# A decoder kernel: grouped attention on four row groups, the next layer's fold inside the experts' routing, mask products not held back

## The chip, the core and the metric

One core of one Trainium2 chip runs the whole program. The metric is the device time of one execution in microseconds; less is better. TensorE does the matrix products, VectorE, ScalarE and GpSimd the rest, SyncE (SP) issues most DMAs.

## What is computed

A decoder of four layers on x of shape (16, 64, 256): in each layer an attention, a second attention against ctx_512 (16, 64, 64) and an expert layer, each added to x after a layer norm. Three of these are touched. The grouped attention, which stands in layer 0 and again in layer 3, has no weights:

```python
def _L3_xattn_ref(q, k, v):            # layer 0 has the same one
    B, S, E, QH, KVH = 2, 256, 256, 32, 8
    D = E // QH                        # 8
    G = QH // KVH                      # 4
    ...
    scores = jnp.einsum('bkgsd,bktd->bkgst', qh, kh) / sqrt(D)
    attn = jax.nn.softmax(scores, axis=-1)
    out = jnp.einsum('bkgst,bktd->bkgsd', attn, vh)
```

Layer 2's expert layer picks one of 32 experts for each token; an expert is a 0/1 mask on one shared ternary weight:

```python
probs = softmax(x @ router_w.T); top1 = argmax(probs)
w_scaled = clip(round(weight / 0.5), -1, 1) * scale
out[token] = probs[top1] * x[token] @ (w_scaled * expert_masks[top1]).T
```

Layer 3's attention needs products of its own weights alone (`Wq_nope` with `Wk`, `Wv` with `Wo`). These are the folds; they depend on no activation.

## The kernel before

The 1024 tokens lie on 128 partitions as NT = 8 tiles of 128 tokens (two sequences of 64 each). The program is a row of eleven stages; a stage is a block in which each engine runs its own instruction list, written out by hand, with semaphores between them. `start_loads(n+1)` puts the loads of the next stage on SP's queue at the start of stage n (L3384), so weights are loaded one stage ahead.

`stage_gqa` (L281) does the grouped attention. For each tile j and TensorE:
- `ask(j)` (L319) transposes the tile's queries into bank 6, as eight products with the identity, 32 columns each on two column groups. ScalarE's `query(j)` copies the bank to `qa`.
- `scores(j, gp)` (L329), twice a tile: scores with the queries as stationary operand, on two row groups of which 32 rows each are used, into banks 0 and 1. They serve only for the row maximum, which VectorE's `top` (L481) takes.
- `tops(j)` (L343) turns the maxima into rows of bank 6; `lift` (L304) copies these rows into `qa` beside the queries, one copy of 8 partitions on ScalarE and one on VectorE.
- `cross(j, b)` (L354), twice a tile: transposed scores with the maximum already subtracted (keys times queries, and a row of -1 times the maximum), four products with 40 rows on two row groups, into banks 2 and 3 for b = 0, banks 4 and 5 for b = 1. ScalarE's `exps` (L444) takes the exponential of two banks.
- `weigh(j, b)` (L367) multiplies with the values on four column groups into bank 7; `pull` copies it out, `bring` (L380) transposes back with four full transposes, VectorE's `finish` (L488) divides and adds to x.

TensorE's order in turn t is `scores(t,0)`, `cross(t-1,0)`, `bring(t-2)`, `scores(t,1)`, `cross(t-1,1)`, `ask(t+1)`, `weigh(t-1,0)`, `tops(t)`, `weigh(t-1,1)` (L388 to L410). GpSimd's `spread` (L416) multiplies the keys with a head mask into `kb`. `hold(k, bank, n)` (L1636) is n filler products whose result nobody reads.

`stage_L2_ffn` (L2078) sorts the tokens by expert: logits (`route_logits`, L1622, the router repeated to 128 columns), softmax and choice on VectorE, ranks as products on TensorE, places on VectorE, then eight indirect DMAs by GpSimd scatter the rows to `sorted_in` (semaphore `sent`). SP waits for `sent` and loads the sorted rows back in groups of two tiles. TensorE then runs `turn(b)` (transposes) and `apply(b)` (two blocks of 64 rows, each with its own masked weight) for 24 tiles. VectorE makes the 48 masked weights (L2295) in a ring of six buffers, and waits for `sent` before the first. Between ranks and `turn(0)` TensorE runs 36 fillers and then the folds `fold_nope(g)` (L2136) and `fold_out(g)` (L2146), g = 0 to 3, behind one wait for all of layer 3's attention loads.

`load_L3_attn` (L1309) issues these loads, `load_gqa` (L261) those of the grouped attention.

## Time and profile before

| | us |
|---|---|
| median of 3 runs | 1398.31 (1396.41 to 1400.75) |
| the profiled execution, its own time | 1398.4 |
| its span, first to last instruction | 1396.7 |
| TensorE busy in the span | 1266.5 (91%) |
| VectorE busy | 778.3 (56%) |
| ScalarE busy | 593.1 (42%) |
| GpSimd busy | 371.0 (27%) |

The span falls into stages that follow one another; the two grouped attentions lie at about 220 to 300 and 1275 to 1353 us, the sorted experts at about 1039 to 1129. A share of busy time over the whole span says nothing of a stage, so the rows further down are taken stage by stage. Rows in order of time merge equal instructions that follow one another; the first column is the start, the second the time from the first start to the last end, and square brackets give the idle time in front and what ended it. A product in fp32 is two records on TensorE. A row of busy time gives the stretch and its length, then busy us (and instructions) of PE, PEld, DVE, ACT and POOL, the granted clock of TensorE as a share of 2.4 GHz, the DMA engines' busy share and GB/s.

### The profile page before, as it was taken

Reading aid. Unit: us, or ns where it says so; the run is one execution under the profiler, and the core shown is the slowest. Engines: PE = TensorE matmul, PEld = TensorE weight load, DVE = VectorE, ACT = ScalarE, POOL = GpSimd, SP = SyncE. Lnnn points to the kernel's source line nnn. Section 1 sums busy time; section 2 is a strip of 40 time slices with the busy share of each in tenths; the row PEclk is TensorE's granted clock in tenths of the full one; section 3 lists DMA queues with packets and bytes.
Section 4 is the critical chain, followed back from the end, with each engine's and each line's share of the span. In section 5 each row is a group of like instructions: output and inputs, shape, how many; then the busy total and the mean of one; then the engine's idle time right before and its main releaser. Section 6 shows DMA issues by size and latency. Waiting matters only on the chain. (4 is left out here: it accounts for less than half of the span.)

```text
span 1396.7 us, 29908 instructions
## 1 busy us (share of the span) xinstructions
PE 1266.5 (91%) x12533; PEld 963.0 (69%) x12533; DVE 778.3 (56%) x1473; ACT 593.1 (42%) x1078; POOL 371.0 (27%) x306
## 2 busy tenths in 40 slices
PE   6989998979989998999988888999988968999988
PEld 3469995558977567788857758788775435676555
DVE  4664565553344572633347655888735675863542
ACT  3632334473555474533332441223433363663451
POOL 0154303015641000555520004444202134523000
PEclk9979999988999999999998988999999999999989
DMA  4000003027006000100056080000016312200000
GB/s 115 1 2 4 4 4 122 1 80 151 1 1 204 1 2 1 35 0 1 1 137 180 1 254 1 2 1 2 2 66 207 124 44 50 55 21 31 2 1 31
DMA packets 78421, 67.81 MB, mean 49 GB/s; under 512 B 22344, under 2 KB 74256, under 8 KB 78160
## 3 DMA queue, kind: packets, MB, share of 16 engines
q1 hardware_dynamic: 75472, 63.10, 15.9%
q8 instruction: 100, 1.64, 0.5%
q0 software_dynamic: 768, 2.10, 0.5%
q10 hardware_dynamic: 2048, 0.70, 0.2%
q14 instruction: 33, 0.27, 0.1%
HBM read 53.30 MB, written 8.39 MB: 44 GB/s over the span
## 5 line engine op out<-in xcount | busy, mean ns | idle before, releaser
L1893 PE MATMUL ps<-rounded 128*128 128x512 f32 x384 | 91.3, 393 | 2.0 <-POOL rounded L1924 1.0
L1296 POOL TENSOR_TENSOR fixed<-fixed,cross 128x768 f32<-128x768 f32 x32 | 58.9, 1841 | 109.5 <-DVE cross L1245 109.5
L1210 PE MATMUL ps<-rounded 128*128 128x256 f32 x576 | 79.8, 294 | 6.8 <-DVE rounded L1264 4.1
L1893 PEld LDWEIGHTS ps<-rounded 128*128 128x128 f32 x384 | 70.9, 188 | 20.4 <-POOL rounded L1924 5.4
L1210 PEld LDWEIGHTS ps<-rounded 128*128 128x128 f32 x576 | 73.5, 197 | 10.9 <-issue 4.7
L1924 POOL TENSOR_TENSOR rounded<-weights,rounded 128x256 fp32r<-128x256 f32 x32 | 23.7, 761 | 185.0 <-ACT rounded L1942 185.0
L211 PE MATMUL ps<-fixed 128*128 128x128 f32 x160 | 35.3, 342 | 39.6 <-ACT fixed L199 30.4
L1275 ACT COPY cross<-ps 128x256 f32<-128x256 f32 x32 | 11.9, 373 | 116.0 <-PE ps L1219 116.0
L211 PEld LDWEIGHTS ps<-fixed 128*128 128x128 f32 x160 | 20.4, 166 | 53.5 <-issue 23.0
L1815 DVE SCALAR_TENSOR_TENSOR fixed<-ps,work,fixed 128x256 f32<-128x256 f32 x64 | 28.0, 479 | 51.5 <-PE ps L1725 51.5
L2031 DVE TENSOR_TENSOR work<-work,ps 128x512 f32<-128x512 f32 x32 | 22.0, 688 | 62.1 <-ACT work L1959 60.0
L1219 PE MATMUL ps<-fixed,work 128*128 128x256 f32 x192 | 50.2, 398 | 6.8 <-POOL fixed L1296 6.4
L1580 POOL TENSOR_TENSOR work<-weights,work 64x512 f32<-64x512 f32 x32 | 41.1, 1286 | 56.9 <-DMA work<-work 32.7
L199 ACT ACTIVATE fixed<-fixed 128x256 f32<-128x256 f32 x96 | 51.9, 592 | 8.1 <-DVE fixed L182 8.0
L485 DVE TENSOR_REDUCE work<-ps 128x16 f32<-128x1024 f32 x32 | 39.1, 1222 | 23.6 <-PE ps L337 23.6
L1745 POOL TENSOR_TENSOR rounded<-work,rounded 128x512 fp32r<-128x512 f32 x32 | 41.1, 1299 | 36.8 <-ACT rounded L1776 36.3
L1725 PEld LDWEIGHTS ps<-rounded 128*128 128x128 f32 x384 | 48.9, 199 | 1.1 <-issue 0.7
L1725 PE MATMUL ps<-rounded 128*128 128x256 f32 x384 | 49.3, 290 | 0.0
L188 ACT ACTIVATE fixed<-fixed 128x2 f32<-128x2 f32 x48 | 13.6, 293 | 80.2 <-DVE fixed L172 77.9
L1912 PEld LDWEIGHTS ps<-rounded 128*128 128x128 f32 x384 | 47.0, 192 | 0.5
L1912 PE MATMUL ps<-rounded 128*128 128x256 f32 x384 | 47.2, 283 | 0.0
L1696 PE MATMUL ps<-rounded 128*128 128x512 f32 x192 | 45.5, 392 | 1.7 <-POOL rounded L1736 1.7
(492 smaller groups left out, 3117.3 us busy)
## 6 DMA issues: line engine op xcount, KB each, us to landing
weights<-in_L_ffn_masksT SPq DMA_DIRECT2D x32, 256.0 KB, 6.5
weights<-in_L_ffn_fc_w SPq DMA_DIRECT2D x16, 256.0 KB
weights<-in_L_xattn_Wq SPq DMA_DIRECT2D x2, 2048.0 KB, 9.8
weights<-in_L_xattn_WoT SPq DMA_DIRECT2D x2, 2048.0 KB, 10.2
work<-work SPq DMA_DIRECT2D x64, 64.0 KB, 2.0
sorted_in<-work SPq DMA_DIRECT2D x1, 3072.0 KB, 14.7
work<-sorted_in SPq DMA_DIRECT2D x12, 256.0 KB, 2.8
sorted_out<-work SPq DMA_DIRECT2D x12, 256.0 KB, 2.2
```

Source lines behind the costliest of these rows:

```text
L199: nc.scalar.activation(to, of, ACT.Identity, bias=k.nshift[:, j:j + 1], scale=k.nrstd[:, j:j + 1]).then_inc(s["n_normed"], 1)
L211: last = nc.tensor.transpose(k.ps[:, banks[i % 2], (2 * c + jj) * P:(2 * c + jj + 1) * P], k.h[:, 2 * i + jj, c * P:(c + 1) * P], k.ident)
L485: nc.vector.tensor_reduce(mx[:, j % 2, gp, :], ps[:, 0:2, :].rearrange("p a (n t) -> p (a n) t", t=SEQ), AX.X, ALU.max).then_inc(s["maxed" ...
L1210: last = nc.tensor.matmul(seen[:, a, :], m[:, u % 2, c, a, :], of[:, c, part * D:(part + 1) * D], start=c == 0 and n == 0, stop=c == KC - ...
L1219: last = nc.tensor.matmul(ps[:, 2, 0:D], c1[:, v // 4, a, :], ro[:, v % 2, a, :], start=a == 0, stop=a == 2)
L1296: nc.gpsimd.tensor_tensor(ro[:, v % 2, :, :], ro[:, v % 2, :, :], sn, ALU.add).then_inc(s["roped"], 1)
L1580: last = nc.gpsimd.tensor_tensor(qb[64:128, 2 * (u % 2) + e, tok], cs[made, v % 2, :], turned_sn[made, v % 2, :], ALU.add)
L1696: last = nc.tensor.matmul(ps[:, 2 * m + half, :], a[:, q % 2, c, :], b[:, c, half * BANK:(half + 1) * BANK], start=c == 0 and part == 0, s ...
L1725: last = nc.tensor.matmul(ps[:, 4 + i, jj * D:(jj + 1) * D], a[:, (e - 1) % 2, c, j * P:(j + 1) * P], b[:, (e - 1) % 2, c, :], start=c == ...
L1745: nc.gpsimd.tensor_tensor(a_rest[:, e % 2, m, tok], act1[:, (4 * e + 2 * m + half) % 3, :], a_top[:, e % 2, m, tok], ALU.subtract).then_in ...
L1893: last = nc.tensor.matmul(ps[:, 2 * (n % 2) + i, :], a[:, q % 2, i, c, :], b[:, c, half * BANK:(half + 1) * BANK], start=c == 0 and part = ...
L1912: last = nc.tensor.matmul(ps[:, 4 + i, jj * D:(jj + 1) * D], a[:, (e - 1) % 2, c, j * P:(j + 1) * P], b[:, (e - 1) % 2, c, :], start=c == ...
```

## The change

In the grouped attention (both uses):
- Keys and queries are laid out in four row groups of 32 partitions in place of two: group r holds in its rows 4 to 19 the 16 numbers of a pair of heads for each of `b`, and in rows 0 to 3 the place for the negated maxima. The rows of ones and the mask now come by DMA: `load_gqa` issues 42 DMAs where it issued 19.
- The normed tile is first copied into a padded buffer `hp` (tile 0 by VectorE, the others by GpSimd); `ask` is then four full transposes, and waits for the padded copy. It moves ahead of `cross(t-1,1)`.
- `scores` uses 64 rows in each of its two row groups; `tops` is eight products on four column groups, with the negated identity `minus`.
- `lift` is four copies of 4 partitions, two on each engine; on VectorE it moves behind `front`, the statistics of the next layer norm.
- `cross` is four products on four row groups into banks 2 to 5, of which b has its half. It waits for the exponentials before it (`2j + b`), where it waited for those before that.
- At the stage's start the fills with -1 and the mask's products go; fills of `hp` with zeros and the first padded copy come.

In the sorted experts: the logits use the 32 router columns once; `fold_nope(0)` moves between logits and ranks, behind a wait for its two loads, which are now the first that `load_L3_attn` issues; the other folds follow the ranks, `fold_out` behind a wait for two further loads; 20 fillers then follow in place of 36 before. VectorE doesn't wait for `sent` any more.

```diff
+    ones, one_hot = d["const_rope64"], d["const_gmask"]
+    for r in range(4):
+        pair, at = r % 2, 32 * r
+        for first, n in ((at, 4), (at + 20, 12)):
+            eng.dma_start(w.keys[first:first + n, :, :, :].rearrange("p b j t -> p (b j) t"),
+                          bass.AP(tensor=ones.tensor, offset=ones.offset, ap=[[0, n], [0, 2 * NT], [1, SEQ]])).then_inc(sem, 16)
+        for first, n, row, col in ((at + 4, 16, 16 * pair, 0), (at + 20, 12, 0, 4)):
+            eng.dma_start(w.gmask[first:first + n, :].rearrange("p (b n) -> p b n", b=2),
+                          bass.AP(tensor=one_hot.tensor, offset=one_hot.offset + 8 * row + col, ap=[[8, n], [0, 2], [1, 4]])).then_inc(sem, 16)
+        for b in range(2):
+            eng.dma_start(w.gmask[at + 2 * b:at + 2 * b + 2, :],
+                          bass.AP(tensor=one_hot.tensor, offset=one_hot.offset + 64 * (4 * b + 2 * pair), ap=[[64, 2], [1, 8]])).then_inc(sem, 16)
+    return 16 * (16 + 2 + 4 * 6)
...
     def lift(eng, copy, s, j, half):
         eng.wait_ge(s["topped"], j + 1)
-        copy(qa[lows[half], j % 3, :, :, :].rearrange("p b g q -> p b (g q)"), bc(ps[lows[half], 6, 0:D], 1, 2)).then_inc(s["lifted"], 1)
+        for low in lows[2 * half:2 * half + 2]:
+            copy(qa[low, j % 3, :, :, :].rearrange("p b g q -> p b (g q)"), bc(ps[low, 6, 0:D], 1, 2)).then_inc(s["lifted"], 1)
+
+    def padded(copy, s, j):
+        copy(hp[:, j % 3, :, :, 4:20], k.h[:, j, :].rearrange("p (g r d) -> p g r d", g=GQA_G, r=4)).then_inc(s["padded"], 1)
...
             def ask(j):
                 if j:
                     pe.wait_ge(s["queried"], j)
+                    pe.wait_ge(s["padded"], j)
+                else:
+                    pe.wait_ge(s["padded0"], 1)
+                if j >= 2:
+                    pe.wait_ge(s["lifted"], 4 * (j - 1))
                 for g in range(GQA_G):
-                    for half in range(2):
-                        at = 64 * g + 32 * half
-                        last = nc.tensor.matmul(ps[64 * half:64 * half + 32, 6, g * P:(g + 1) * P], k.h[:, j, at:at + 32],
-                                                k.ident, start=True, stop=True, tile_position=(0, 64 * half))
+                    last = nc.tensor.transpose(ps[:, 6, g * P:(g + 1) * P], hp[:, j % 3, g, :, :].rearrange("p r d -> p (r d)"), k.ident)
                 last.then_inc(s["asked"], 1)
...
+                pe.wait_ge(s["minus"], 1)
                 for gp in range(2):
-                    for half in range(2):
-                        last = nc.tensor.matmul(ps[lows[half], 6, gp * P:(gp + 1) * P], mx[:, j % 2, gp, 8 * half:8 * half + 8],
-                                                k.ident, start=True, stop=True, tile_position=(0, 64 * half + 32))
+                    for r in range(4):
+                        last = nc.tensor.matmul(ps[lows[r], 6, gp * P:(gp + 1) * P], mx[:, j % 2, gp, 4 * r:4 * r + 4],
+                                                minus, start=True, stop=True, tile_position=(0, 32 * r))
                 last.then_inc(s["topped"], 1)
 
             def cross(j, b):
-                pe.wait_ge(s["lifted"], 2 * j + 2)
-                if j:
-                    pe.wait_ge(s["expd"], 2 * j - 1 + b)
-                for pair in range(2):
-                    for half in range(2):
-                        rows = slice(64 * half, 64 * half + 40)
-                        last = nc.tensor.matmul(ps[:, 2 + 2 * b + half, pair * D:(pair + 1) * D],
-                                                kb[rows, 2 * j + b, 2 * pair:2 * pair + 2, :].rearrange("p n t -> p (n t)"),
-                                                qa[rows, j % 3, b, :, :].rearrange("p g q -> p (g q)"),
-                                                start=True, stop=True, tile_position=(64 * half, 0))
+                pe.wait_ge(s["lifted"], 4 * j + 4)
+                if 2 * j + b:
+                    pe.wait_ge(s["expd"], 2 * j + b)
+                for r, rows in enumerate(groups):
+                    pair = r % 2
+                    last = nc.tensor.matmul(ps[:, 2 + r, b * D:(b + 1) * D],
+                                            kb[rows, 2 * j + b, 2 * pair:2 * pair + 2, :].rearrange("p n t -> p (n t)"),
+                                            qa[rows, j % 3, b, :, :].rearrange("p g q -> p (g q)"),
+                                            start=True, stop=True, tile_position=(32 * r, 0))
                 last.then_inc(s["crossed"], 1)
...
+                if t + 1 < NT:
+                    ask(t + 1)
                 if 1 <= t <= NT:
                     cross(t - 1, 1)
-                if t + 1 < NT:
-                    ask(t + 1)
...
+            nc.gpsimd.memset(hp[:, 1:3, :, :, :], 0.0).then_inc(s["hzero"], 1)
             pool.wait_ge(w.sem, w.loaded)
-            pool.wait_ge(s["minus"], 2)
-            pool.wait_ge(s["masked"], 3)
             spread(0)
+            pool.wait_ge(s["hzero"], 1)
+            for j in range(1, 3):
+                padded(nc.gpsimd.tensor_copy, s, j)
...
                 spread(j)
+                if j + 1 < NT:
+                    pool.wait_ge(s["asked"], j - 1)
+                    if j == 2:
+                        pool.wait_ge(s["padded0"], 1)
+                    padded(nc.gpsimd.tensor_copy, s, j + 1)
...
-                nc.scalar.activation(pT[:, b, :, :].rearrange("p m q -> p (m q)"),
-                                     ps[:, 2 + 2 * b:4 + 2 * b, :].rearrange("p a q -> p (a q)"), ACT.Exp,
-                                     scale=scale).then_inc(s["expd"], 1)
+                nc.scalar.activation(pT[:, b, :, :],
+                                     ps[:, 2:6, b * D:(b + 1) * D], ACT.Exp, scale=scale).then_inc(s["expd"], 1)
...
+            nc.vector.memset(hp[:, 0, :, :, :], 0.0).then_inc(s["hzero0"], 1)
+            dve.wait_ge(s["hzero0"], 1)
+            nc.vector.tensor_copy(hp[:, 0, :, :, 4:20], k.h[:, 0, :].rearrange("p (g r d) -> p g r d", g=GQA_G, r=4)).then_inc(s["padded0"], 1)
+            nc.vector.tensor_scalar(minus, k.ident, -1.0, None, ALU.mult).then_inc(s["minus"], 1)
...
                 if t < NT:
                     top(t, 1)
-                    lift(dve, nc.vector.tensor_copy, s, t, 1)
                 if t >= 2 and t % 2:
                     front((t - 3) // 2)
+                if t < NT:
+                    lift(dve, nc.vector.tensor_copy, s, t, 1)
...
+    w.keys_sem, w.values_sem = k.nc.alloc_semaphore("L3_keys_weights"), k.nc.alloc_semaphore("L3_values_weights")
+    eng.dma_start(w.kT, d[p + "WkT"]).then_inc(w.keys_sem, 16)
+    eng.dma_start(w.qnT, d[p + "Wq_nopeT"]).then_inc(w.keys_sem, 16)
+    eng.dma_start(w.vT, d[p + "WvT"]).then_inc(w.values_sem, 16)
+    eng.dma_start(w.wo, d[p + "Wo"].rearrange("(h p) d -> p h d", p=P)).then_inc(w.values_sem, 16)
+    eng.dma_start(w.all, d[p + "Wall"].rearrange("(c p) s -> p c s", p=P)).then_inc(sem, 16)
     eng.dma_start(w.rot, d[p + "Wq_rot"][0:P]).then_inc(sem, 16)
     eng.dma_start(w.rot_low, d[p + "Wq_rot"][P:192]).then_inc(sem, 16)
-    eng.dma_start(w.all, d[p + "Wall"].rearrange("(c p) s -> p c s", p=P)).then_inc(sem, 16)
-    eng.dma_start(w.qnT, d[p + "Wq_nopeT"]).then_inc(sem, 16)
-    eng.dma_start(w.kT, d[p + "WkT"]).then_inc(sem, 16)
-    eng.dma_start(w.vT, d[p + "WvT"]).then_inc(sem, 16)
-    eng.dma_start(w.wo, d[p + "Wo"].rearrange("(h p) d -> p h d", p=P)).then_inc(sem, 16)
...
             pe.wait_ge(w.sem, w.loaded)
-            route_logits(k, pe, w.router, E, s["logits"])
+            for j in range(NT):
+                for c in range(KC):
+                    last = nc.tensor.matmul(ps[:, 6 + j // 4, (j % 4) * P:(j % 4) * P + E], k.hT[:, c, j * P:(j + 1) * P], w.router[:, c, :],
+                                            start=c == 0, stop=c == KC - 1)
+            last.then_inc(s["logits"], 1)
+            pe.wait_ge(k.next.keys_sem, 32)
+            fold_nope(0)
             pe.wait_ge(s["order"], 3)
             pe.wait_ge(s["sel"], 1)
...
             last.then_inc(s["ranks"], 1)
-            hold(k, 4, 36)
-            pe.wait_ge(k.next.sem, k.next.loaded)
+            for g in range(1, 4):
+                fold_nope(g)
+            pe.wait_ge(k.next.values_sem, 32)
             for g in range(4):
-                fold_nope(g)
                 fold_out(g)
+            hold(k, 4, 20)
             pe.wait_ge(s["noped"], 4)
             pe.wait_ge(s["pms"], 4)
             turn(0)
@@ -2198,6 +2229,7 @@
                 for made, rows, half in ((k.next.nope, slice(0, P), 0), (k.next.low, slice(64, P), 1)):
                     ins = nc.scalar.copy(made[rows, 2 * g:2 * g + 2, :].rearrange("p u d -> p (u d)"), ps[rows, 2 + g % 2, half * D:half * D + D])
                 ins.then_inc(s["noped"], 1)
+            for g in range(4):
                 act.wait_ge(s["pm"], g + 1)
                 nc.scalar.copy(k.next.pm[:, 2 * g:2 * g + 2, :].rearrange("p a d -> p (a d)"), ps[:, g % 2, :]).then_inc(s["pms"], 1)
             copy_turned(0)
@@ -2287,7 +2319,6 @@
             chain.step(nc.vector.tensor_reduce(passed[row], past[row], AX.X, ALU.add))
             nc.vector.tensor_scalar(table[row], passed[row], E - 1.0, float(KC * D), ALU.min, ALU.mult).then_inc(s["table"], 1)
             dve.wait_ge(s["table"], 1)
-            dve.wait_ge(s["sent"], 16 * NT)
```

## Rows read from the trace of the kernel before

**Rows 1.** Order of time, turn t=5 of the first attention: start us, us, engine, line.
```profile
263.08 1.13 PE L337 MATMUL ps<-work 32*128 32x256 f32 x8
...
264.26 1.23 DVE L485 TENSOR_REDUCE work<-ps 128x16 f32<-128x1024 f32 x1 [1.28 <-PE ps L337]
...
265.21 0.66 PE L383 MATMUL ps<-fixed,work 128*128 128x128 f32 x4
265.33 1.02 ACT L448 ACTIVATE work<-ps 128x1024 f32<-128x1024 f32 x1 [1.52 <-PE ps L361]
...
265.80 1.13 PE L337 MATMUL ps<-work 32*128 32x256 f32 x8
...
266.76 0.42 DVE L495 TENSOR_TENSOR fixed<-fixed,work 128x256 f32<-128x256 f32 x1
...
266.86 1.14 PE L361 MATMUL ps<-work 40*128 40x256 f32 x8
...
267.92 0.95 PE L325 MATMUL ps<-fixed 128*32 128x128 f32 x13
...
269.04 0.58 ACT L441 COPY work<-ps 96x512 f32<-96x512 f32 x1 [2.69 <-PE ps L325]
...
269.72 0.61 PE L350 MATMUL ps<-fixed,work 128*8 128x128 f32 x8 [0.30 <-issue]
270.37 0.70 DVE L306 COPY work<-ps 8x512 f32<-8x512 f32 x1 [2.05 <-PE ps L350]
...
270.59 0.64 PE L375 MATMUL ps<-work 128*32 128x256 f32 x8 [0.27 <-ACT work L448]
...
271.16 1.13 PE L337 MATMUL ps<-work 32*128 32x256 f32 x8
```

**Rows 2.** Busy time per engine, granted clock (PEclk), DMA, over the first attention's loop.
```profile
231.00:291.00 60.00, 55.07 (x548) 33.52 (x548) 33.97 (x56) 31.68 (x41) 2.05 (x3) 1.00 0.11 35
```

**Rows 3.** Order of time, the edges of the first attention stage.
```profile
220.87 0.91 DVE L501 MEMSET weights<- 32x1024 f32 x1 [1.67 <-PEq L78]
...
224.93 1.13 PE L337 MATMUL ps<-work 32*128 32x256 f32 x8
...
238.84 1.13 PE L337 MATMUL ps<-work 32*128 32x256 f32 x8
...
285.95 1.13 PE L361 MATMUL ps<-work 40*128 40x256 f32 x8
```

**Rows 4.** Order of time, the sorted experts up to their first tile.
```profile
1039.75 5.34 PE L1626 MATMUL ps<-fixed 128*128 128x128 f32 x32 [0.93 <-PEq L78]
...
1050.11 0.37 PE L2160 MATMUL ps<-work 128*128 128x256 bf16 x1 [5.02 <-DVE work L1606]
...
1061.23 1.54 PE L2141 MATMUL ps<-weights 128*128 128x64 f32 x13 [1.08 <-DMA fixed<-in_L_attn_kv_norm_w]
...
1068.05 5.14 SPq L2221 DMA_DIRECT2D work<-sorted_in  x5
...
1072.17 0.85 PE L2120 MATMUL ps<-fixed,work 128*128 128x128 f32 x6 [0.72 <-issue]
```

**Rows 5.** One line's operations (mask products): ns min/median/max, first and last start.
```profile
L2295 DVE TENSOR_TENSOR work<-weights,fixed x48: 691/693/695, 1069.1 to 1107.5; 128x512 f32<-128x512 f32 x48
```

**Rows 6.** Busy time, clock, DMA share and GB/s while the next layer's weights load.
```profile
1041.00:1047.00 6.00, 4.09 (x28) 3.90 (x27) 2.60 (x6) 0.42 (x1) 0.34 (x1) 0.84 1.00 337
```

**Rows 7.** The page's DMA issues: count, KB each, median us from issue to landing.
```profile
work<-sorted_in SPq DMA_DIRECT2D x12, 256.0 KB, 2.8
```

**Rows 8.** Order of time, GpSimd's scatter and gather beside VectorE's operations.
```profile
1054.52 1.74 DVE L2286 TENSOR_TENSOR work<-work 1x1536 f32<-1x1536 f32 x1
1054.92 2.43 POOL L2245 DMA_INDIRECT sorted_in<-fixed,work  x1 [13.57 <-DVE work L2283]
...
1115.29 0.95 POOL L2250 DMA_INDIRECT work<-sorted_out,work  x1 [0.30 <-issue]
1115.60 0.48 DVE L2299 SCALAR_TENSOR_TENSOR fixed<-work,fixed 128x256 f32<-128x256 f32 x1 [7.44 <-DMA work<-sorted_out,work]
```

35 lines of the change are left out of this document (14 added, 21 removed).

## The prediction

> **What bounds the kernel now.** I read the order of time in three places: one turn of the grouped attention's loop, that stage's edges, and the start of the sorted experts. The busy time of two stretches, one line's operations and one row of the DMA issues answer what is left.
>
> In the loop [rows 1] one turn lasts 271.16 - 263.08 = 8.08 us, and TensorE starts a new group as soon as the last one lets it: `scores` 1.06 (265.80 to 266.86), `cross` 1.06 (266.86 to 267.92), `bring` with four full transposes 0.59 (265.21 to 265.80), `weigh` 0.57 (270.59 to 271.16). Two `scores`, two `cross`, one `bring` fill 4.83. `ask` from 267.92 is in VectorE's and ScalarE's chain: its end lets ScalarE copy the queries (269.04 to 269.62), that lets `tops` start (269.72), that the lift (270.37). VectorE's `top` takes 1.23, the exponentials 1.02. So TensorE bounds the loop, with about half a us of waiting in front of `tops`. The granted clock is full there (1.00, the 2.4 GHz level) [rows 2].
>
> The edges: the loop begins at 224.93, its third turn at 238.84 (13.9 us for two turns, the first behind fillers, the second behind the load of the exponential's table), and the last tile's `cross` is at 285.95 [rows 3]. In between there are five full turns (t = 2 to 7): 238.84 + 5 x 8.08 = 279.24.
>
> In the sorted experts [rows 4] the chain is: logits to 1045.1, VectorE's routing, ranks on TensorE at 1050.11, places, the scatter, its landing, `turn(0)`. The folds for the next layer begin at 1061.23, when the last of that layer's loads lands, and run on one after another until `turn(0)` at 1072.17. After it the 48 mask products (0.693 each, 1069.1 to 1107.5 [rows 5]) set the pace: 38.4 us over 47 steps, 0.817 a product, 1.63 for the two of a tile.
>
> **Part 1, the attention, step by step.** Seen from TensorE's turn:
> - `cross`: four products, before on two row groups (two rounds, 1.06), now on four (one round). No row of before has four row groups of 128 columns. From below by the count of rounds: half the streaming goes. `weigh` has the same moving width (256) and one round on four column groups, 0.57 [rows 1], so a round beyond the first costs 1.06 - 0.57 = 0.49 at most. Bounds: 0.57 and 1.06. I take 0.63, near `weigh`, because the pair on two row groups already runs together (the same 1.06 does for four products).
> - By the Trainium skill, TensorE: Matmul & The Clock Gate, Part 3 (Measured speedup vs the span model), four row groups gave 3.07 times, not 4. By it the round would be about 0.1 longer, the turn about 0.25, the sum about 2.5 smaller. No run here shows it yet.
> - `ask`: eight narrow products become four full transposes, as `bring`: 0.59 for 0.68 or so. It moves ahead of `cross(t-1,1)`, which takes ScalarE's copy off the way to `tops`.
> - Lift: two copies become four, two on each engine. A copy of 4 partitions is as long as one of 8, so VectorE's becomes 0.70 x 2 = 1.40 [rows 1].
> - Padded copies on GpSimd: some 256 elements a tile; its eight spreads leave it idle for most of the loop. Nothing, as long as it is a tile ahead; exposed it would be about a us a turn.
> - `cross` now waits for the preceding exponentials, since all four banks are shared. Between two `cross` there are `bring`, `scores`, `ask`, 2.2 us, against 1.02: free in the loop.
>
> The new turn, from `scores(t,0)` = 0: `cross(t-1,0)` 1.06 to 1.69, `bring` to 2.28. `top(t,0)` starts at 1.18 (as 264.26 after 263.08) and ends at 2.41, and only then may `scores(t,1)` start: 2.52, a wait that is new, to 3.58. `ask` to 4.17, query copy to 4.87. `cross(t-1,1)` to 4.80, exponentials 4.92 to 5.94, `weigh` to 5.37. `top(t,1)` ends at 4.99 (VectorE does the finish of an older tile first, from 2.45: it takes 1.31, as from `bring`'s end at 265.87 to 267.18), so `tops` goes at 5.37 to 5.94. `weigh(t-1,1)` 5.98 to 6.55. The turn is **6.55**, 1.53 less. Lifts: 6.05 to 7.45; they release `cross(t,0)` at 7.56, it is due at 6.55 + 1.06 = 7.61. So there is 0.05 of room: VectorE's lift is what comes next.
>
> Five turns give 5 x 1.53 = 7.65. The first two together give 0.5: the lift is exposed there (0.4 to 0.5 lost) and ScalarE's table load goes 0.6 later, while the earlier `ask` and shorter `cross` give 1.4 back. The last turn loses 0.9: it has no `scores` after the lift, and VectorE's norm statistics (1.05) now stand ahead of the lift, so the last tile's `cross` comes 7.6 after the turn's start, not 6.71. The tail behind it, two `cross` and two exponentials in series, is 0.2 shorter. Start: the fills and mask products go (0.91 of VectorE for 1024 columns [rows 3]), but `ask(0)`, which before waited for nothing in the stage, waits for a fill of 512 (half of that, 0.46) and a copy of 256 columns (0.42, as 266.76): 1.0 later with the releases, and with half the matmuls 0.4 to 0.9 shorter: 0.3 lost. One stage: 7.65 + 0.5 - 0.9 + 0.2 - 0.3 = 7.15. **Two stages: 14.3.**
>
> The load of the stage has 23 more DMAs on SP's queue. At some 0.35 to 0.7 us to issue each that is 8 to 16 us; it is issued a whole stage earlier, and nothing in the rest of those stages starts that soon. Nothing; exposed it would be those 8 us once.
>
> **Part 2, the fold and the logits.** Logits with 32 columns in place of 128: the rate there is 5.34/32 = 0.167 a record over both clock levels; the fold's products, with 64 columns, take 1.54/13 = 0.118, tail included [rows 4]. The stretch from 1041 shows 337 GB/s [rows 6]: 2.1/0.337 = 6.2, landed at 1047.3 to 1048. The fold takes 1.9, so it ends at 1049.5 or so, ahead of the ranks at 1050.11. Queued behind it on TensorE are the ranks, and VectorE waits for those. Bounds: 0.4 gained, 1.5 lost; I take 0. The other folds and 20 fillers end by about 1067. Then `turn(0)` no longer waits for folds but for the first sorted rows, issued at 1068.05 [rows 4] and some 3 us to landing (2.8 [rows 7]): 1071.1 for 1072.17, **1.0 gained**. But TensorE now idles for 3 to 4 us before it, where the folds ran right up to it. If the clock falls to its 1.2 GHz level, the first tiles cost up to 1.5 more. I take 1.0 lost.
>
> **Part 3, the mask products ahead.** Six buffers, so six products (4.4 us) can be done early. Before, they were done at 1073.9, and the seventh waits for the first tile's products at 1074.2: the gain is 0.3 unless the first tile comes earlier. The 42 others go at 0.817 from then. What it can cost is the scatter: [rows 8] the first scatter DMA took 2.43 on GpSimd, from 1054.92, beside a VectorE product with two SBUF inputs that ended at 1056.26; but the gather's took 0.95 with such an operation of 0.48 inside it, neither one longer. So an issue that starts within a product may wait for its end (0.3 on average, at most four issues) and one that is under way does not: 0 to 4.2 (all six products), I take 0.8. The Trainium skill, SBUF — State Buffer (SBUF: two separate sides), says that of a VectorE operation with two SBUF inputs and a GpSimd operation that reads SBUF, the one that starts first has the port pair for its whole length; the first row agrees, the gather's do not. By it the scatter would be some 4 us later.
>
> Parts 2 and 3: 1.0 + 0.3 - 1.0 - 0.8 = -0.5.
>
> **Sum.** 14.3 - 0.5 = 13.8. The profiled execution took 1398.4 (span 1396.7 and 1.7 around it), 0.1 above the median of 1398.31. 1398.4 - 13.8 = **1384.6**.
>
> **Rivals.**
> - *Four row groups run as two rounds.* Then `cross` stays at 1.06; the order alone gives a turn of 7.2, 0.88 less, so 5 x 0.88 + 0.5 - 0.9 - 0.1 = 3.9 a stage less 0.3: 7.2 for both. 1391.7. For it: no row shows four. Against: the column groups. 12%.
> - *Scatter and products block each other* (mechanism above, in full). Each issue waits for a product and the clock falls as well: 4 us more than I took: 1388.6. For it the 2.43, against it the gather. 14%.
> - *The lift sets the turn.* If VectorE's two copies or an exponential over four banks are 0.3 longer, `cross` waits 0.3 a turn: 5 x 0.3 x 2 = 3: 1387.6. 10%.
> - *Slower: the clock falls inside the loop.* The shorter groups leave TensorE waiting in front of `scores(t,1)` and `weigh`. At 1.2 GHz each round streams twice as long: 2 x 1.91, 2 x 1.06, five of 1.0: 10.9 a turn. Above a share of (8.08 - 6.55)/(10.9 - 6.55) = 35% of the loop at that level the change loses; with both loops at it throughout, 1384.6 + 10 x 4.35 = 1428. Against: 1.00 now [rows 2], with the half us of waiting per turn there already. 4%.
> - *It doesn't do what it says*: padded copies or added loads bound the stage instead, and the gain is gone: 1398. 4%.
>
> Forecast 56%, between 1381 and 1387.
>
> **Numbers.** The range reaches from 1380.5 (both folds' gains, no cost of parts 2 and 3) to 1391.5 (most of the first three rivals). Within 0.3% (4.2 us, about what can be told from no change): 1394 to 1402.5. Faster 0.87, same 0.08, slower 0.05.
>
> **What would show it.** Right: a turn near 6.5 between two `scores(t,0)`, the `cross` group 0.6 long with its four weight loads together, `scores(t,1)` released by `top`, ranks at 1050, `turn(0)` after its rows' landing. Wrong: `cross` still 1.06, a wait on the lift in front of `cross(t,0)`, scatter issues of over 1 us, or a low granted clock in either loop. What would make the number wrong most easily is the 0.05 us of room at the lift, and the clock at `turn(0)`.

## The result and the profile after

| | before | changed |
|---|---|---|
| median, same chip | 1397.36 us (1392.70 to 1400.75, 4 runs) | 1377.30 us (1375.72 to 1380.95, 4 runs) |
| ratio, 95% interval | 1 | 0.9856 (0.9828 to 0.9884) |

The change is faster by 20 us, with 16 to 24 in the interval. Forecast were 13.8 us less and a range down to 1380.5; the time lies 3.2 us below that range. The profiled execution took 1375.72.

The changed kernel's page: span, busy time, and the granted clock in 40 slices (tenths).

```profile
span 1374.0 us, 29841 instructions
...
PE 1243.2 (90%) x12453; PEld 947.3 (69%) x12453; DVE 790.8 (58%) x1487; ACT 602.8 (44%) x1094; POOL 376.5 (27%) x320
...
PEclk9989999989999999999998989999996999999989
```

The slice of 6 at about 1030 us is the start of the sorted experts, at half clock.

The changed kernel in order of time, one steady turn of the first attention (answers to [rows 1]): `scores` is L358, `cross` L380, `bring` L402, `ask` L346, `weigh` L394, `tops` L370, the lift L321, `top` L509.

```profile
247.68 1.42 DVE L321 COPY work<-ps 4x512 f32<-4x512 f32 x2 [0.17 <-PE ps L370]
...
248.32 1.13 PE L358 MATMUL ps<-work 64*128 64x256 f32 x8
...
249.38 0.31 PEld L380 LDWEIGHTS ps<-work 32*128 32x128 f32 x8 [0.33 <-DVE work L321]
249.38 0.71 PE L380 MATMUL ps<-work 32*128 32x256 f32 x8
249.50 1.22 DVE L509 TENSOR_REDUCE work<-ps 128x16 f32<-128x1024 f32 x1 [0.41 <-PE ps L358]
...
250.03 0.65 PE L402 MATMUL ps<-fixed,work 128*128 128x128 f32 x4
...
250.87 1.14 PE L358 MATMUL ps<-work 64*128 64x256 f32 x8 [0.19 <-DVE work L509]
...
251.94 0.66 PE L346 MATMUL ps<-fixed,work 128*128 128x128 f32 x4
...
252.52 0.71 PE L380 MATMUL ps<-work 32*128 32x256 f32 x8
...
253.17 0.64 PE L394 MATMUL ps<-work 128*32 128x256 f32 x8
253.30 1.02 ACT L473 ACTIVATE work<-ps 128x1024 f32<-128x1024 f32 x1
...
253.62 0.62 PE L370 MATMUL ps<-work 128*4 128x128 f32 x16
...
254.31 1.42 DVE L321 COPY work<-ps 4x512 f32<-4x512 f32 x2 [1.04 <-PE ps L370]
...
254.38 0.64 PE L394 MATMUL ps<-work 128*32 128x256 f32 x8
...
254.95 0.49 PE L358 MATMUL ps<-work 64*128 64x256 f32 x2
```

The turn is 254.95 - 248.32 = 6.63 us. `cross` holds TensorE 0.65 (249.38 to 250.03). The wait forecast as new is there, 0.19 behind `top`. So is the lift's: 247.68 + 1.42 = 249.10, and `cross` starts at 249.38, just as `scores` lets it go. The loop's clock stayed full (answers to [rows 2]):

```profile
230.00:283.00 53.00, 46.15 (x525) 25.93 (x525) 39.64 (x71) 36.90 (x53) 4.20 (x6) 1.00 0.05 17
```

The changed kernel in order of time, the sorted experts up to the first tile (answers to [rows 4] and [rows 8]).

```profile
1024.55 7.01 PE L2183 MATMUL ps<-fixed 128*128 128x32 f32 x32 [0.93 <-PEq L78]
...
1032.00 3.02 PE L2165 MATMUL ps<-weights 128*128 128x64 f32 x16 [0.44 <-DMA weights<-in_L_attn_Wq_nopeT]
...
1036.57 0.37 PE L2190 MATMUL ps<-work 128*128 128x256 bf16 x1 [1.55 <-DVE work L1630]
...
1041.38 2.44 POOL L2277 DMA_INDIRECT sorted_in<-fixed,work  x1 [15.23 <-DVE work L2315]
...
1045.74 0.69 DVE L2326 TENSOR_TENSOR work<-weights,fixed 128x512 f32<-128x512 f32 x1 [1.03 <-issue]
...
1046.88 0.69 DVE L2326 TENSOR_TENSOR work<-weights,fixed 128x512 f32<-128x512 f32 x1 [0.44 <-issue]
1047.72 2.90 DVE L2326 TENSOR_TENSOR work<-weights,fixed 128x512 f32<-128x512 f32 x4
1047.91 1.33 POOL L2277 DMA_INDIRECT sorted_in<-fixed,work  x1 [0.30 <-issue]
...
1049.55 1.17 POOL L2277 DMA_INDIRECT sorted_in<-fixed,work  x1 [0.30 <-issue]
...
1054.71 4.03 SPq L2253 DMA_DIRECT2D work<-sorted_in  x5
...
1057.73 1.20 PE L2144 MATMUL ps<-fixed,work 128*128 128x128 f32 x6 [1.76 <-DMA work<-sorted_in]
...
1060.98 1.45 DVE L2326 TENSOR_TENSOR work<-weights,fixed 128x512 f32<-128x512 f32 x2 [10.36 <-PE ps L2155]
```

Counted from the first logit product, before and after: logits 5.34 and 7.01 us long, ranks at 10.36 and 12.02, first scatter at 15.17 and 16.83, `turn(0)` at 32.42 and 33.18. Between these two executions the stage lost 2.6 us.

**Where the 22.7 us between the two profiled spans lie.** Counted from TensorE's first product of one stage to that of the next, some 9 of them lie in stages whose code is the same in both kernels. The first attention, to the next stage's logits, went from 79.4 to 72.2, near the 7.15 less of the forecast. But the L0 experts behind it took 107.9 for 111.1, the L1 stage 144.7 for 145.6, the last layer's attention 143.4 for 145.3, and the L0 attention ahead of it all 200.8 for 203.9. This count puts the start of each grouped attention, up to its own first product, into the stage ahead of it, and that start is 5.17 us with the new code for 3.69 (first attention; 2.73 for 1.73 at the second). Counted from the last product ahead of the stage, the first attention gave 5.8 us (77.3 for 83.1) and the second 7.7 (72.5 for 80.3), and the unchanged code is nearly 12 us shorter, 4.6 of it in the L0 attention (195.6 for 200.2).

Three theories. A: my sum stands, and what the unchanged stages gave is not the change's. B: a shorter attention moves the low stretches of TensorE's clock in what follows. C: one execution's luck. Every kernel below has a trace, and so one more execution of the unchanged stages.

### The profile page after: what moved, and what is told of

Same layout as the page of the kernel before. It is cut to its first block and busy times, and to the rows that moved or that the text cites. A ratio compares the mean times of both kernels' runs of the same rounds, so it can differ in the third digit from the quotient of the medians.

```text
span 1374.0 us, 29841 instructions
## 1 busy us (share of the span) xinstructions
PE 1243.2 (90%) x12453; PEld 947.3 (69%) x12453; DVE 790.8 (58%) x1487; ACT 602.8 (44%) x1094; POOL 376.5 (27%) x320
## 3 DMA queue, kind: packets, MB, share of 16 engines
q1 hardware_dynamic: 78096, 63.63, 16.3%
## 5 line engine op out<-in xcount | busy, mean ns | idle before, releaser
L1917 PE MATMUL ps<-rounded 128*128 128x512 f32 x384 | 91.1, 393 | 2.0 <-POOL rounded L1948 1.0
L1298 ACT COPY cross<-ps 128x256 f32<-128x256 f32 x32 | 11.9, 372 | 115.3 <-PE ps L1242 115.3
L509 DVE TENSOR_REDUCE work<-ps 128x16 f32<-128x1024 f32 x32 | 39.2, 1224 | 18.2 <-PE ps L358 17.6
```

Of the source, the lines that this page charges most:

```text
L509: nc.vector.tensor_reduce(mx[:, j % 2, gp, :], ps[:, 0:2, :].rearrange("p a (n t) -> p (a n) t", t=SEQ), AX.X, ALU.max).then_inc(s["maxed" ...
L1917: last = nc.tensor.matmul(ps[:, 2 * (n % 2) + i, :], a[:, q % 2, i, c, :], b[:, c, half * BANK:(half + 1) * BANK], start=c == 0 and part = ...
```

## The experiments

**b_attn, b_experts: the halves of the change.** b_attn is the kernel before with the diff's attention part (its functions `load_gqa` and `stage_gqa`); b_experts is the kernel before with the rest.

> The kernel before with the attentions' part of the change alone (four row groups, padded copies, earlier ask, new loads); the sorted experts, their fold and the order of the last layer's loads are as before. Theory A, my forecast's own sum: 14.3 us less than before (about 1383), so the 20 us come mostly from elsewhere. Theory B, the trace of after: the two attention stages give 13.9 to 14 and the stages that were not changed give the rest (L0 attention 4.7, L0 experts 3.8, L3 attention 2 to 3 shorter), because TensorE's low-clock stretches fall elsewhere once the attention is shorter; then this kernel alone is 20 to 23 us faster than before (about 1375 to 1377). Theory C: the shorter unchanged stages are one execution's luck in where the low clock falls; then this kernel's profile has L0 attention and L0 experts nearer to before, and its median gain is 14 to 17.

Measured: 1377.98 against 1395.01, ratio 0.9890 (0.9866 to 0.9915): 15.3 us less, 11.9 to 18.7.

> The kernel before with the rest of the change alone: logits of 32 columns, the first fold ahead of the ranks, loads reordered, mask products not waiting for the scatter. The attentions are as before, so its trace up to 1040 us is a second execution of unchanged code. My forecast: 0.5 us slower. By the trace of after (that stage 92.85 us for 90.2): 2.6 slower. A rival: the reordered loads make the last layer's attention shorter by 2 to 3, so the sum is 0. Theory C (luck of the low clock): its stages ahead of 1040 us differ from before's by some us in places although nothing is changed there; otherwise each agrees within 0.5.

Measured: 1396.58 against 1395.01, ratio 1.0000 (0.9976 to 1.0023).

So the attention is the whole gain, and the other two parts are worth nothing within some 3 us. The interval holds A's 14.3 and C's 14 to 17, and not B's 20. C is right about one stage: the L0 attention took 203.9 in before and 200.2 in b_experts, with the same code. It comes in two courses: with low clock from 60 us after its start for 17 us and also at 16, or only from 56 to 59 on, for 14 or 17 us. Of all 14 profiled executions three took the long one: before, b_dense (204.2, old attention) and a_logits128 (205.2, new). What separates the two courses, 3.7 us between before and b_experts, is the execution's own. The L0 experts' are not, as the table further down shows, and there B holds, with a smaller amount.

**b_order: the loop's order alone.**

```diff
+                if t + 1 < NT:
+                    ask(t + 1)
                 if 1 <= t <= NT:
                     cross(t - 1, 1)
-                if t + 1 < NT:
-                    ask(t + 1)
...
-                    lift(dve, nc.vector.tensor_copy, s, t, 1)
                 if t >= 2 and t % 2:
                     front((t - 3) // 2)
+                if t < NT:
+                    lift(dve, nc.vector.tensor_copy, s, t, 1)
```

> The kernel before with only the order of the attention's loop as changed: ask(t+1) ahead of cross(t-1,1) on TensorE, VectorE's norm statistics ahead of the lift; cross on two row groups, fills, masks and loads as before. By my forecast's working for a second round in cross, the order alone gives a turn of 7.2 for 8.08, so 5 x 0.88 x 2 = 8.8 less the last turn's 0.9 x 2: 7 us faster than before. If instead the turn's gain came from the row groups (two cross of 1.06 become 0.64, 0.84 a turn) and the order gives only what is left of 1.45, the turn is 7.47 and the kernel 4 to 5 us faster. If both are needed together (VectorE's chain sets the turn unless cross is short), the turn stays within 0.2 of 8.08.

Measured: 1386.93 against 1396.30, ratio 0.9931 (0.9905 to 0.9957), 9.6 less (6.0 to 13.3). b_order in order of time, TensorE, one turn:

```profile
241.96 1.13 PE L337 MATMUL ps<-work 32*128 32x256 f32 x8
...
246.73 1.13 PE L361 MATMUL ps<-work 40*128 40x256 f32 x8
247.79 0.64 PE L375 MATMUL ps<-work 128*32 128x256 f32 x8
248.26 0.61 PE L350 MATMUL ps<-fixed,work 128*8 128x128 f32 x8
248.99 0.64 PE L375 MATMUL ps<-work 128*32 128x256 f32 x8
249.56 0.70 PE L337 MATMUL ps<-work 32*128 32x256 f32 x4
```

The turn is 249.56 - 241.96 = 7.60, not 7.2: of the 1.45 that a turn gained, 0.48 is the order and 0.97 the rest of the attention's change: the row groups with their two shorter `cross` (0.82), and what goes with them. From the last product ahead of the stage to the next stage's first logits it takes 81.55 for 84.41, and 77.55 for 80.25 at the second attention (b_fill's, below, whose attentions are as before): 5.6 us for both. That is nearer to the second expectation (a turn of 7.47, 4 to 5 us) than to my 7; the whole came out lower still, with an end of its interval at 6.0.

**a_logits128, a_fold_late, a_fold_late2: what the routing's start costs.** a_logits128 is the changed kernel with the logits on 128 columns:

```diff
-            for j in range(NT):
-                for c in range(KC):
...
-            last.then_inc(s["logits"], 1)
+            route_logits(k, pe, w.router, E, s["logits"])
```

> The changed kernel with the router's logits computed on 128 (repeated) columns again, all else as changed. In the trace of after, the stage's first 24 us ran at the 1.2 GHz level and the logits took 7.0 us for 5.34 before. If the narrow products keep the clock low: the logits take 5.3, the level is back at 1.00 within them, the ranks come 1.7 earlier, the folds run at full clock, and the whole is 1.7 to 3 us faster than the changed kernel (1374 to 1375.6). If the clock is low there for another reason (what ran before the stage), the logits get longer, by up to 0.5 us, and the whole is the same or slower by 0.5.

Measured: 1377.56 against 1395.01, ratio 0.9872 (0.9848 to 0.9897); not told apart from the changed kernel's. a_logits128 in order of time:

```profile
1028.12 5.45 PE L1650 MATMUL ps<-fixed 128*128 128x128 f32 x32 [0.93 <-PEq L78]
...
1036.96 3.01 PE L2165 MATMUL ps<-weights 128*128 128x64 f32 x16 [3.39 <-DMA weights<-in_L_attn_Wq_nopeT]
...
1039.90 0.39 PE L2186 MATMUL ps<-work 128*128 128x256 bf16 x1
```

The logits are back at 5.45. Over all profiled executions they took 5.3 to 5.5 with 128 columns and 6.2 to 7.0 with 32. But the ranks came only 0.24 earlier, at 11.79 after the first logit product, now held by something else: `fold_nope(0)` waited 3.39 for its load, ran 3.0 at half clock, and the ranks stood behind it with no idle time.

a_fold_late moves that fold behind the ranks, to the other three, with 36 fillers for 20 ahead of `turn(0)`; a_fold_late2 is the same with 16.

```diff
-            pe.wait_ge(k.next.keys_sem, 32)
-            fold_nope(0)
             pe.wait_ge(s["order"], 3)
...
-            for g in range(1, 4):
+            pe.wait_ge(k.next.keys_sem, 32)
+            for g in range(4):
                 fold_nope(g)
...
-            hold(k, 4, 20)
+            hold(k, 4, 36)
```

> The changed kernel with logits of 128 columns and fold_nope(0) behind the ranks (with the other folds), 36 fillers for 20 ahead of turn(0). In a_logits128 fold_nope(0) waited 3.4 us for its load at 8.84 after the first logit product, ran at the 0.5 level, and the ranks stood behind it until 11.79, for 10.36 in before. Theory: ranks at 10.4 to 10.5, the scatter's end 1.3 earlier, turn(0) at 31.6 instead of 32.9, the seventh mask product at 33.7 instead of 35.1 (full level at turn(0)), so 1.3 us faster than a_logits128 (about 1376). Rival: the rows' landing or the sorted rows' load sets turn(0) all the same: no change.

Measured: 1380.30 against 1396.30, ratio 0.9896 (0.9869 to 0.9923). a_fold_late in order of time, TensorE:

```profile
1034.04 0.37 PE L2184 MATMUL ps<-work 128*128 128x256 bf16 x1 [5.02 <-DVE work L1630]
...
1035.21 11.52 PE L2165 MATMUL ps<-weights 128*128 128x64 f32 x61
...
1051.35 7.72 PE L1663 MATMUL ps<-fixed 128*128 128x512 bf16 x35 [0.16 <-issue]
1058.90 0.82 PE L2144 MATMUL ps<-fixed,work 128*128 128x128 f32 x6
```

The ranks are at 10.47, 1.3 earlier, as expected; `turn(0)` is at 35.3, not 31.6, because my 36 fillers stood in front of it for 7.7 us.

> a_fold_late with 16 fillers in place of 36 ahead of turn(0). There the ranks came at 10.47 and the last scatter issue ended at 27.14 after the first logit product, as expected, but the fillers ran from 27.8 to 35.3 and turn(0) stood behind them. With 16 they end at 31.2 to 31.4; turn(0) goes with its rows' landing at 31.6 to 31.9, and the seventh mask product at 33.7 to 34.0, for 35.1 in a_logits128 and a_sent: 1.2 us faster than these by the trace in this stage, at most 1376 to 1377 for the whole (less than the timing can tell from the changed kernel). Rival: the load of the first sorted rows lands later than 31.9 whatever the scatter does; then turn(0) stays near 32.9.

Measured: 1376.03 against 1395.88, ratio 0.9856 (0.9826 to 0.9886), again not told apart from the changed kernel. `turn(0)` at 33.24 and the seventh mask product at 35.31: neither is earlier than a_logits128's 32.89 and 35.12. Not the rows' load (the rival) held it: TensorE was never idle there. Four folds behind the ranks ended at 30 us, and the 16 fillers (3.4) behind them set `turn(0)`. The earlier ranks were given back to the folds. So the fold ahead of the ranks takes 1.3 from the routing and gives them back later; between the two places there is nothing to gain as long as folds and fillers fill the time up to `turn(0)`. The kernel with the late fold and no fillers was not run. In a_logits128 `turn(0)` came 4.4 us after the last scatter issue's end (28.49); by that the rows of a_fold_late2 (27.02) were there at an estimated 31.4, nearly 2 us before its `turn(0)`.

**a_sent: the wait for the scatter put back.**

```diff
             dve.wait_ge(s["table"], 1)
+            dve.wait_ge(s["sent"], 16 * NT)
```

> The changed kernel with VectorE's wait for the end of the scatter put back ahead of the mask products. Contention theory at its full price (4 us): 4 us faster than the changed kernel, scatter issues of 0.95. By the trace of after (issues of 0.96 to 1.33, 0.6 over in all): the scatter ends 0.6 earlier, turn(0) 0.6 earlier, but the six products are late and the seventh is where it was: within 0.5 us of the changed kernel. My forecast's numbers: 0.8 back and 0.3 lost, so 0.5 faster.

Measured: 1378.94 against 1395.01, ratio 0.9894 (0.9870 to 0.9917). a_sent in order of time, its sixth and seventh scatter issues and first mask products:

```profile
1047.21 0.96 POOL L2277 DMA_INDIRECT sorted_in<-fixed,work  x1 [0.30 <-issue]
1048.47 0.96 POOL L2277 DMA_INDIRECT sorted_in<-fixed,work  x1 [0.30 <-issue]
...
1053.22 0.69 DVE L2327 TENSOR_TENSOR work<-weights,fixed 128x512 f32<-128x512 f32 x1 [10.46 <-issue]
```

Without mask products beside them all seven later issues take 0.96; in the changed kernel two of seven took 1.33 and 1.17, so 0.58 in all. In each of the six other kernels with the early products it was two as well, 0.5 to 0.6 in all. They are the two that start within a mask product: the issue of 1047.91 has 0.50 of a product left and is 0.37 longer, that of 1049.55 has 0.34 left and is 0.21 longer. In b_experts it is the third and the fifth of the seven, with 0.54 and 0.31 left, 0.41 and 0.18 longer. The others start while no product runs; products begin inside them and lengthen neither side, 0.96 and 0.69. That is the mechanism on which my 0.8 rested. The first issue's 2.43 is there with and without mask products; it always starts within the product of 1.74 on one partition (L2318 here), which no run takes away. By the Trainium skill, SBUF — State Buffer (SBUF: two separate sides), whichever of a VectorE operation with two SBUF inputs and a GpSimd operation that reads SBUF starts first has the shared port pair for the whole instruction. The issues that start within a product agree; the products that start within an issue and take 0.69 all the same do not, and the 4 us that the prediction drew from that rule are excluded here. The last mask product starts at 68.67 after the first logit product in a_sent and at 68.56 in a_logits128: the early products bring nothing, the contention costs nothing.

**a_shift, a_period, b_shift: fillers that only move what follows.** An edge is here the moment at which the granted clock goes from one of its levels to the other. In all 14 traces the low stretches (1.2 GHz) last 3.41 us or a multiple (6.83, 10.24, 13.65, 17.07, 23.89, 27.31; only the last one is cut off by the trace's end), and within a trace all edges lie whole steps of that length apart. Where they fall on a stage depends on how long the stages ahead took. The three kernels add fillers to the first turn of both attentions' loops and nothing else, to 16 (a_shift) and 22 (a_period) in the changed kernel and to 19 in the kernel before (b_shift):

```diff
                 if t == 0:
-                    hold(k, 4, 6)
+                    hold(k, 4, 16)
```

> The changed kernel with ten more fillers (2.1 us) in the first turn of both attentions' loops, which only makes each attention stage 2.1 us longer and so moves what follows against the grid of 3.41 us on which the granted level changes. Phase theory: what stands between the L0 experts' 107.9 behind the new attention and 109.4 to 111.1 behind the old one is where that grid falls on the stage; with the edge moved from 0.8-1.6 (mod 3.41, counted from the first logit product) to 2.1-2.9 the low stretch at 22 to 25 is 6.8 to 10.2 us for 3.4, and the stage takes 109.4 to 111. The kernel is then 4.2 us slower for its fillers and 1.5 to 3 more. Content theory (the new attention leaves something that helps the stage, whatever the grid): 107.9 as before, 4.2 slower.

> The changed kernel with 16 more fillers in the first turn of both attentions' loops: by a_shift's 2.07 us for ten, each attention stage is 3.3 to 3.5 us longer, which is one whole period of the grid of 3.41 us on which the granted level changes. Grid theory: the L0 experts' stage is back at 107.9 (a low stretch of 3.4 us at 24.5 to 25.5 after the first logit product), L1_both at 144.6, as without fillers, and the kernel is 6.8 us slower than the changed one (1384 to 1385), faster than a_shift's 1388 although its stages hold 2.6 us more of fillers. Rival (longer attention, or fillers there, cost what follows): L0 experts 111 or more, 1391.

> The kernel before with 13 more fillers in the first turn of both attentions' loops (2.7 to 2.8 us each). In b_experts and b_fill, with the old attention, the level is back 3.7 us after the first logit product and low again at 24.1 for 6.8 us (stage 109.4 to 109.5). Grid theory: 2.75 us more put these edges at 4.4 (mod 3.41), where they are with the new attention; low for 3.4 us at 24.7 to 24.9, the stage takes 107.9, and L1_both 144.6 for 145.6 to 146.6: 2.7 of the 5.5 us that the fillers cost come back, so 2.5 to 3 slower than before. Content theory (the old attention leaves the stage at 109.4 to 111): 5.5 slower.

Granted clock, from 21 to 33 us after the first logit product of the L0 experts (stretch, length, busy us of the engines, then the clock): the kernel before, b_experts, the changed one, a_shift, a_period and b_shift.

```profile
321.03:333.03 12.00, 11.07 (x38) 9.30 (x39) 4.50 (x7) 0.43 (x2) 4.45 (x5) 0.57 1.11 191
```
```profile
318.83:330.83 12.00, 12.00 (x60) 10.92 (x61) 5.24 (x10) 0.00 (x0) 3.51 (x4) 0.72 1.14 195
```
```profile
310.50:322.50 12.00, 11.62 (x67) 10.72 (x68) 6.15 (x13) 0.00 (x0) 3.86 (x4) 0.86 1.08 180
```
```profile
312.13:324.13 12.00, 11.13 (x38) 9.34 (x39) 4.44 (x7) 0.37 (x2) 4.37 (x5) 0.57 1.07 200
```
```profile
314.16:326.16 12.00, 11.78 (x68) 10.67 (x69) 6.15 (x13) 0.00 (x0) 3.74 (x4) 0.86 1.10 190
```
```profile
319.86:331.86 12.00, 11.83 (x68) 10.70 (x69) 6.13 (x13) 0.00 (x0) 3.67 (x4) 0.86 1.06 203
```

With 0.57, 10.2 of the 12 us are at the 1.2 GHz level; with 0.72, 6.8; with 0.86, 3.4. Its price, in the changed kernel and a_shift in order of time, the eight bias products (16 records), the same code:

```profile
310.88 3.77 PE L1734 MATMUL ps<-weights,work 8*128 8x256 f32 x16 [1.30 <-DVE work L1828]
```
```profile
313.00 6.52 PE L1734 MATMUL ps<-weights,work 8*128 8x256 f32 x16 [1.30 <-DVE work L1828]
```

All profiled executions, from the first product of a stage to that of the next (for the L0 experts: from the first product behind the logits):

| kernels | attention | full clock again, us after the first logit product | low again | L0 experts | L1 |
|---|---|---|---|---|---|
| before; b_dense | old | 5.6; 5.7 | 22.7, 10.2 us; (26.2, 6.8) | 111.1; (111.7) | 145.6; 144.9 |
| b_experts, b_fill, b_order | old | 3.7, 3.7, 2.8 | 24.1, 24.2, 23.3, 6.8 us | 109.4 to 109.5 | 145.7 to 146.6 |
| b_shift | old, 2.8 us longer | 4.0 | 24.5, 3.4 us | 107.9 | 144.5 |
| changed, b_attn, a_sent, a_fold_late, a_fold_late2, a_logits128 | new | 4.0 to 5.0 | 24.5 to 25.5, 3.4 us | 107.8 to 107.9 | 144.5 to 144.8 |
| a_shift | new, 2.1 longer | 5.5 | 22.6, 10.2 us | 111.2 | 145.5 |
| a_period | new, 3.5 longer | 4.1 | 24.6, 3.4 us | 107.9 | 144.5 |

(b_dense has fillers of its own in that stage.) Ordered by where the clock falls, the executions are in order of time, whichever attention stands ahead: at 22.6 and 22.7 it stays low for 10.2 us, at 23.3 to 24.2 for 6.8, at 24.5 to 25.5 for 3.4. The stage's time goes with the edge alone. The old attention, 2.8 us longer, gives 107.9; the new one, 2.1 longer, gives 111.2, and 3.5 longer, one step, 107.9 again. Content theory would have left the old at 109 or more and the new at 107.9. It falls.

The whole times: a_shift 1388.25, ratio 0.9938 (0.9910 to 0.9966); a_period 1387.25 (1383.07 to 1387.71), ratio 0.9926 (0.9900 to 0.9952); b_shift 1396.83 against 1395.88, ratio 0.9994 (0.9976 to 1.0013). b_shift's upper end, 1.8 slower, excludes the 5.5 of its fillers unpaid, and also misses my 2.5 to 3. The whole times of a_shift and a_period are not told apart by their intervals, so they do not show the step back that the stage shows. a_shift's profiled span is 1387.0, 13.0 over the changed kernel's, of which the fillers are 2 x 2.07 = 4.1, the L0 experts 3.3 and L1 0.8; the second attention without its fillers 2.3 (79.93 - 2.07 - 75.56), the last layer's attention 2.7 (146.0 for 143.35), both with more low clock (17.1 us for 10.2, and 13.7 for 3.4). So I had counted the edges' price in two stages only, and it is paid in more. Part of this is the changed kernel's one execution: five others with the new attention and without added fillers have 143.7 to 145.1 for its 143.35. By the medians a_shift is 11 us slower than the changed kernel, 7 beyond its fillers. a_period's profiled execution fits (span 1381.3, 7.3 over); its median does not, 2 to 3 above what I expected. The profiled execution is the fastest of six, and the others have no trace: inconclusive on the whole, clear on the stage.

**b_fill, b_dense: why the clock falls there.** Six fillers in each of the two gaps of the L0 experts (b_fill); six in the second gap and two behind each of the first three pairs of bias products (b_dense, without the diff's first edit; the last edit is b_dense's alone).

```diff
+                        if q == 1:
+                            hold(k, 2, 6)
                         pe.wait_ge(s["w_rest"], q + 1)
...
                     last.then_inc(s["combT"], 1)
+                    hold(k, 4, 6)
                     pe.wait_ge(s["cT"], 1)
...
                         last.then_inc(s["bias"], 1)
+                        if i < 3:
+                            hold(k, 7, 2)
```

> The kernel before with six fillers on TensorE in each of the two gaps of the L0 experts' stage (1.4 us at 12.0 after the first logit product, where it waits for the second weights' rest, and 1.3 at 20.6, where it waits for the copy of the combination weights); nothing else is changed. Theory: these gaps let the granted level fall to 0.5 at 22.7 (10.2 us of it in before, 6.8 in b_experts, 3.4 in each kernel with the new attention), and this is the 2 to 3 us that the unchanged stage is shorter behind the new attention. Then no low stretch follows here and the stage, from its first full product's marker to the next stage, takes 107 to 108 us for 111.1 and 109.4; the kernel is 1.5 to 3.5 us faster than before. Rival: the low level has another cause; then it still falls at about 22 to 25 and the time is that of before.

Measured: 1394.24 against 1396.30, ratio 0.9981 (0.9963 to 1.0000). Low from 24.2 for 6.8 us, stage 109.5: as b_experts, to 0.1. TensorE was idle for no more than 0.05 us at a time from 16.3 us on, and its clock fell all the same, amid the bias products. At this edge the gaps are not the cause; the rival holds. Of before's edge, where the clock falls earlier (22.7), this run says nothing. What moved the whole by 2 us, if anything did, the trace doesn't show.

> The kernel before with 12 fillers in the L0 experts' stage: six in the 1.3 us gap at 19.7 to 21.0 after the first logit product (as in b_fill) and two after each of the first three pairs of bias products, which contract over 8 rows only and fill TensorE from 21 to 25.1. In b_fill the gaps were filled and the level was still low from 24.2 for 6.8 us. Theory: it is the products over 8 rows (after the eight transposes to 8 partitions) that do not hold the level, busy as TensorE is; with full products of 128 rows between them the low stretch is gone or 3.4 us shorter, and the stage takes 107.9 to 109 for 109.5, the fillers' 1.3 us included. Rival: fillers among them change nothing, low for 6.8 us or more again, the stage at 110.5 or above. The whole stays within 2 us of before in either case; the stage's own time and the granted level decide.

Measured: 1397.90 against 1396.59, ratio 0.9997 (0.9976 to 1.0018). This execution has before's course and edge (5.7), so it stands against before's 22.7 and 10.2 us: low now from 26.2, for 6.8. b_dense in order of time, TensorE, its last bias products:

```profile
325.73 1.13 PE L1711 MATMUL ps<-weights,work 8*128 8x256 f32 x4
326.79 1.03 PE L1639 MATMUL ps<-fixed 128*128 128x512 bf16 x2
327.75 2.07 PE L1711 MATMUL ps<-weights,work 8*128 8x256 f32 x4
```

At one edge the clock held one step longer with full products among those over 8 rows; the last two of these (four records), which have no fillers behind them, fell into the low stretch and take 2.07 for 1.13. The expected 3.4 us less of low clock came, the shorter stage didn't (111.7 with 2.6 us of fillers, for 111.1). This is one execution at one edge, and b_dense also fills the gap ahead of the bias products. No execution has that filler alone at this edge, so which of the two fillings held the clock is open. The products over 8 rows are a possible cause, not a shown one.

## Why the prediction was too high

**Right, in its steps.** The turn: 6.63 for a forecast 6.55, against 8.08. The term reads, forecast and measured: `cross` 0.63 and 0.65; `ask` 0.59 and 0.58; `scores(t,1)` at 2.52 and 2.55 behind `top`; lift 1.40 and 1.42; exponentials from 4.92 and 4.98, which carries the last 0.08. The rival of two rounds (`cross` at 1.06) is out, and so is the clock falling in the loop (1.00). That the lift would set the turn is also out, though narrowly: `cross` starts 0.28 behind the lift's end, at its own pace behind `scores`. In the first turn, where the lift is the last to come, `cross` follows its end by 0.05 (229.12 to 229.17), so the room is some 0.2 where 0.05 was forecast. The Trainium skill, TensorE: Matmul & The Clock Gate, Part 3 (Measured speedup vs the span model), has four row groups (32 rows, 512 columns) at 3.07 times. For products of 256 columns the rows show 1.06 for two rounds and 0.65 for one; with the 0.1 more that the prediction estimated from the page the turn would have been 6.8, and it is 6.63.

Per stage, by the four stretches of the sum:

| | forecast | measured, b_attn against b_fill |
|---|---|---|
| first two turns | -0.5 | -1.1 and -0.9 (14.15 and 13.90 to 13.04) |
| five turns | -7.65 | -7.25 (40.40 to 33.15) |
| last turn and tail | +0.7 | +0.5 (20.79 to 21.29) |
| start, from the last product ahead of the stage | +0.3 | +0.6 and +1.6 (9.06 and 5.16 to 9.63 and 6.72) |
| both stages | -14.3 | -7.3 and -6.0 = -13.3 |

So the mechanism was right and single terms were off: the first two turns gave twice the forecast, the start cost two to five times. In two other executions with the new attention (the changed kernel's, a_fold_late's) the second start is 5.04, which makes the sum 15.0: the eight fillers ahead of the loop take 3.2 us at half clock in b_attn and 1.9 at full clock in these, and again the edge decides. The whole times of b_attn, 11.9 to 18.7 less, hold all of this. The 23 more DMAs on SP's queue cost nothing that the traces show, as forecast: up to its last product the L0 attention, in which they are issued, takes 195.2 to 196.7 us in its usual course with the old loads and 195.4 to 196.6 with the new.

Parts 2 and 3, 0.5 lost by forecast, 0 within 3 us by measurement. The terms: contention 0.8, measured 0.6; the mask products early 0.3, measured 0.1 or nothing; `turn(0)` freed from folds, right (it waited 1.76 for its rows). "Between nothing and 1 us gained; I take nothing" for the narrow logits went the other way, 0.8 to 1.7 lost, near the bound of 1.5. The fold ahead of the ranks, taken at 0 because it ends at 9.8: its load landed at 7.5 to 8.8 rather than 7.6 to 8.3, it took 3.0 at half clock rather than 1.9, and it ended at 11.8 in a_logits128; 1.3 lost, also near its bound. (In the changed kernel itself the fold ended at 10.5 and the ranks waited 1.55 for VectorE behind it; there the narrow logits are the loss, and the two don't add up.) Both were paid back by slack later in the stage: from the first logit product to the next stage it was 90.2 to 92.9 us with the old code and 91.1 to 93.2 with the new.

**Wrong: what surrounds the sum.** The prediction costed the edited stages and left the others as they were. Two terms were missing.
- *The start of the subtraction.* I subtracted from 1398.4, the profiled execution, since it was 0.1 from a median of three. The kernel before, timed again on four occasions (13 to 23 runs each), had medians of 1395.0, 1396.3, 1395.9 and 1396.6. The profiled one had taken the long course through the L0 attention, 203.9 for 200.2. Against 1396 the forecast would have been 1382.2: 2.4 us. (Against the 1397.36 of the result's own four runs the term is 1.0.)
- *Unchanged stages.* An attention that is 7 us shorter makes the clock's edges fall elsewhere on what follows: 1.6 to 3.3 us in the L0 experts, 0.1 to 2.1 in L1 (145.6 to 146.6, and 144.9 in b_dense, against 144.5 to 144.8). Some 3 us for the usual course. The three shifted kernels show, in the traces of these stages, that this is where the edge falls, and not the edit. The whole times alone don't show the 3 us: b_attn's interval holds the sum with them and without.

1384.6 - 2.4 - 3 = 1379.2. About 2 us to 1377.3 are left open, which is within the interval.

The range erred in the same way: its bounds came from edited terms alone (4 us to one side), while the edges' place was worth 9 us over the kernel in a_shift's profile (13.0 longer for 4.1 us of fillers) and 7 by the medians. The lower bound is also not the sum that it names: without the costs of parts 2 and 3 (1.8) and with the gains of logits and fold (1.0 and 0.4) it is 1381.4, not 1380.5.
